# Gates in one write, a ninth offset on the other diagonal, and a router in token halves: new instruction orders in a fused vision-transformer kernel

## What is computed

```python
t = unfold3x3(x)                         # [16, 3136, 64*9]
h1 = relu(t @ W1 + b1); s = sigmoid(h1 @ W2 + b2)
h = (t * s) @ W3 + b3                    # tokenizer
h = concat([cls_tok, h])                 # 3137 tokens
u = rmsnorm(layernorm(h)); q, k, v = u @ w_qkv; q, k = elu(q) + 1, elu(k) + 1
a = layernorm(h) + (q @ sum(k v^T)) / (q @ sum(k)) @ w_out + b_out   # 8 heads of 8
h = h + a + rmsnorm(a, w_norm2)
y = layernorm(h)
top2 = top_k(softmax(relu(y @ rw1 + rb1) @ rw2 + rb2), 2); g = softmax(top2)
h = h + sum over 2 of 6 experts: g_e * (relu(relu(y @ e1) @ e2) @ e3 + b)
```

## Time and profile before

| | us |
|---|---|
| median of 3 runs (2600.67 to 2604.88) | 2604.82 |
| the profiled execution, its own time | 2603.84 |
| its span, first to last instruction | 2602.1 |
| mean granted TensorE clock (1.00 is full speed) | 0.906 |

### The profile page before, as it was taken

The page is one execution under the profiler, slowest core; times in us unless marked ns, Lnnn a source line. Parts: engine busy times, 40 slices in busy tenths (PEclk is TensorE's granted clock), DMA queues, the critical chain, the costliest instruction groups (busy, mean ns, idle before and its releaser), DMA issues. The chain is left out here.

```text
span 2602.1 us, 36855 instructions
## 1 busy us (share of the span) xinstructions
PE 2135.0 (82%) x12353; PEld 921.4 (35%) x12353; DVE 1350.6 (52%) x3631; ACT 1103.6 (42%) x2213; POOL 511.4 (20%) x346
## 2 busy tenths in 40 slices
PE   7888878888878888888888888888888888876665
PEld 2333433333333333333334333333333333333322
DVE  4454646454545555564646464646464645544442
ACT  3443434444444444343534444444444444433233
POOL 1112212121221212122212121212121212121110
PEclk9998989899999989899989998999899999977777
DMA  2112222313131312222222222232313131211122
GB/s 106 61 61 63 63 71 53 84 46 91 46 91 46 88 49 80 57 69 68 69 68 67 71 66 71 57 81 56 81 46 91 46 91 46 51 43 43 44 48 58
DMA packets 41339, 168.30 MB, mean 65 GB/s; under 512 B 6048, under 2 KB 19264, under 8 KB 33984
## 3 DMA queue, kind: packets, MB, share of 16 engines
q1 hardware_dynamic: 41152, 165.95, 23.6%
HBM read 151.87 MB, written 14.05 MB: 64 GB/s over the span
## 5 line engine op out<-in xcount | busy, mean ns | idle before, releaser
L1243 DVE TENSOR_TENSOR gh<-f,gate_sp 128x448 f32<-128x448 f32 (+1 forms) x342 | 199.8, 612 | 436.5 <-issue 360.9
L682 ACT ACTIVATE th<-ps,b_half 128x448 f32<-128x448 f32 x504 | 294.8, 630 | 171.8 <-PE ps L354 106.4
L810 ACT ACTIVATE f<-ps,packed 128x448 f32<-128x448 f32 (+1 forms) x342 | 201.1, 630 | 371.9 <-DVE gh L1243 371.2
L920 DVE SCALAR_TENSOR_TENSOR gated<-th,x_tile 128x448 f32<-128x448 f32 x504 | 301.0, 617 | 16.3 <-PE ps L370 7.9
L388 PE MATMUL ps<-packed,rx_c 112*128 112x112 f32 (+1 forms) x225 | 56.7, 407 | 303.7 <-DVE rx_c L930 303.7
L856 POOL TENSOR_TENSOR rstd_u<-var_u,exponent 112x8 f32<-112x8 f32 (+1 forms) x57 | 92.3, 1619 | 1003.2 <-DVE var_u L946 1003.2
L326 PE MATMUL ps<-x_tile,packed 128*64 128x448 f32 x896 | 256.5, 693 | 2.0 <-DMA x_tile<-x_rows 2.0
L354 PE MATMUL ps<-h,packed 64*128 64x448 f32 x896 | 229.1, 588 | 9.8 <-ACT h L674 6.9
L370 PE MATMUL ps<-gated,w_half 128*64 128x448 f32 x896 | 203.7, 557 | 34.0 <-DVE gated L920 34.0
L856 POOL TENSOR_TENSOR rms_b<-ms_b,exponent 112x8 f32<-112x8 f32 (+1 forms) x57 | 107.3, 1882 | 591.2 <-DVE ms_b L1102 591.2
L610 PE MATMUL ps<-gh,packed 128*64 128x448 f32 (+1 forms) x684 | 216.7, 731 | 5.3 <-DVE gh L1243 5.3
(11 more groups left out here) (140 smaller groups left out, 3344.1 us busy)
## 6 DMA issues: line engine op xcount, KB each, us to landing
gate_sp<-gates_d SPq DMA_DIRECT2D x112, 672.0 KB, 7.0
x_tile<-x_rows SPq DMA_DIRECT2D x56, 696.0 KB, 5.2
x_tile<-x_rows SPq DMA_DIRECT2D x56, 580.0 KB, 3.8
out<-out_t SPq DMA_DIRECT2D x56, 224.0 KB, 8.1
gates_d<-gates_c SPq DMA_DIRECT2D x224, 5.2 KB
packed<-pack SPq DMA_DIRECT2D x1, 690.0 KB, 9.8
packed<-pack SPq DMA_DIRECT2D x1, 448.0 KB, 6.5
packed<-pack SPq DMA_DIRECT2D x1, 430.0 KB, 3.6
```

The lines of the kernel that those rows point to most:

```text
L682: act.activation(th[(u + s) % 4][:, :], bank(S0 + u % 2), ACT.Tanh, bias=b2_half[:, m:m + 1], scale=0.5).then_inc(th_set, 1)
L810: act.activation(f2[j % 4][:, 0:n], bank(S0 + j % 2, n), ACT.Relu, bias=cst("eb2")[:, j:j + 1]).then_inc(f2_set, 1)
L920: dve.scalar_tensor_tensor(as_rows(gated[u % 4][:, :]), as_rows(th[(u + s) % 4][:, :]), 1.0, x_view(s, u), ALU.add, ALU.mult).then_inc(gat ...
L1243: dve.tensor_tensor(gh[j % 4][:, 0:n], f2[j % 4][:, 0:n], gate_sp[:, j, 0:n], ALU.mult).then_inc(gh_set, 1)
```

## The change

- `save_gates` is one DMA. The experts are sorted for it in the weights (`rw2`, `eb3`, `order` swap neighbours for image 1), `spread_gates` reads every second row, and `gate_hidden` picks its row accordingly.
- SyncE's order is write, output store, broadcast, x load. It was store, x load, write, broadcast.
- The ninth offset of w1, w2 and w3 takes the other diagonal of the array, for which its pixels are on the other image's partitions. center_a, q_prod, out_proj and center_b become two quadrant products each on the first diagonal.
- The router's product is made in two halves of the tokens (224 each) on four strips of 32 columns, `rh` is 128 x 224, and the logits are four products of 64 rows into two banks, M0 and D1 (banks D0 and D1 change places so that these two are neighbours). The router's bias is added on VectorE, into SBUF, which makes 21 gate operations.
- The banks' waits follow: `kv_prod` and `attention` wait for that addition in the place of `att_set` for D1, `logits` waits for `att_set`.
- The orders of all engines are new. In the diff their old lines are left out; of ScalarE's order the first part is shown.

```diff
-                for img in range(2):
-                    for low in range(2):
-                        top = (low + img) % 2
-                        sp.dma_start(gates_d[f % 2][top * E + img:top * E + E:2, 0:nt * tw],
-                                     gates_c[img * E + low:img * E + E:2, 0:nt * tw]).then_inc(gate_saved, 16)
+                sp.dma_start(gates_d[f % 2][:, 0:nt * tw], gates_c[:, 0:nt * tw]).then_inc(gate_saved, 16)
...
-                    rows = gates_d[f % 2][top * E:top * E + E, 0:n]
+                    rows = gates_d[f % 2][top:2 * E:2, 0:n]
...
+                if 1 <= step - 10 <= CLS_T: save_gates(step - 10)
+                if 1 <= step - 12 <= CLS_T: store_out(step - 12)
+                if 1 <= step - 10 <= CLS_T: spread_gates(step - 10)
+                if 3 <= step + 2 <= BLOCKS: load_x(step + 2)
...
-                        pe.matmul(as_rows(bank(L0, p0=64 * img, p1=64 * img + 64)), cst("w1", 4 * C)[half(img)],
-                                  x_view(s, UNITS - 1)[half(img)], start=False, stop=True).then_inc(w1_done, 1)
+                        pe.matmul(as_rows(bank(L0, p0=64 * img, p1=64 * img + 64)), cst("w1", 4 * C)[half(1 - img)],
+                                  x_view(s, UNITS - 1)[half(1 - img)], start=False, stop=True).then_inc(w1_done, 1)
...
-                pe.matmul(bank(L1, nt * tw), cst("center"), h_of(r, 0)[:, 0:nt * tw], start=True,
-                          stop=True).then_inc(ctr_done, 1)
+                for img in range(2):
+                    pe.matmul(ps[half(img), L1, 0:nt * tw], cst("center")[half(img)], h_of(r, 0)[half(img), 0:nt * tw],
+                              start=True, stop=True).then_inc(ctr_done, 1)
...
+                w = min(n, N // 2)
+                for part in range((nt + 1) // 2):
+                    for img in range(2):
+                        p0 = 2 * RH * part + RH * img
+                        mm = pe.matmul(ps[p0:p0 + RH, M0, 0:w], cst("rw1")[half(img)],
+                                       y[f % 2][half(img), part * w:(part + 1) * w], start=True, stop=True)
+                        if part == (nt + 1) // 2 - 1:
+                            mm.then_inc(router_done, 1)
...
+                if f + 1 <= BLOCKS:
+                    pe.wait_ge(att_set, 2 * (f + 1))
+                    pe.wait_ge(clsatt_set, (f + 1 - 1) // CHUNKS + 1)
+                elif 1 <= f - 1:
+                    pe.wait_ge(gate_step, GATE_STEPS * (f - 1 - 1) + 1)
+                for k in sorted(range(nt), key=lambda k: k % 2):
+                    mm = pe.matmul(ps[0:tw, LOGIT[k // 2], 2 * E * (k % 2):2 * E * (k % 2 + 1)],
+                                   rh[half(k // 2), k % 2 * tw:(k % 2 + 1) * tw], cst("rw2")[half(k // 2)],
+                                   start=True, stop=True)
+                    if k >= nt - 2:
+                        mm.then_inc(logit_done, 1)
...
@@ the order of TensorE @@
             for step in STEPS:
+                if 1 <= step - 9 <= CLS_T: out_proj(step - 9)
+                if 0 <= step - 2 <= BLOCKS: q_prod(step - 2); kv_prod(step - 2)
+                if 1 <= step - 1 <= BLOCKS: w2(step - 1, 3); w3(step - 1, 1); w3(step - 1, 2); w2(step - 1, 4)
+                if 1 <= step - 1 <= BLOCKS: w3(step - 1, 3)
+                if 1 <= step - 9 <= CLS_T: mean_sq_b(step - 9)
+                if 0 <= step - 2 <= BLOCKS: spread_hn(step - 2)
+                if 1 <= step - 10 <= CLS_T: gates_channels(step - 10)
+                if 1 <= step - 1 <= BLOCKS: w3(step - 1, 4)
+                if 0 <= step - 2 <= BLOCKS: kv_outer(step - 2)
                 if 1 <= step - 11 <= CLS_T: out_tokens(step - 11)
+                if 1 <= step - 10 <= CLS_T: expert_h1(step - 10, 0)
+                if 1 <= step - 8 <= BLOCKS: attention(step - 8)
                 if 1 <= step - 9 <= CLS_T: spread_b(step - 9)
+                if 1 <= step - 10 <= CLS_T: expert_h1(step - 10, 1); expert_h2(step - 10, 0)
                 if 1 <= step - 9 <= CLS_T: center_b(step - 9)
+                if 1 <= step - 10 <= CLS_T: expert_h1(step - 10, 2); expert_h2(step - 10, 1)
                 if 1 <= step - 9 <= CLS_T: var_mean_b(step - 9)
+                if 1 <= step <= BLOCKS: w1(step, 0); w1(step, 1); w1(step, 2); w1(step, 3)
                 if 0 <= step - 1 <= BLOCKS: center_a(step - 1)
+                if 1 <= step <= BLOCKS: w1(step, 4)
+                if 1 <= step - 10 <= CLS_T: expert_h2(step - 10, 2); expert_bias(step - 10)
                 if 1 <= step - 9 <= CLS_T: spread_c(step - 9)
+                if 0 <= step - 1 <= BLOCKS: var_mean_a(step - 1)
                 if 1 <= step - 10 <= CLS_T: expert_out(step - 10, 0)
+                if 1 <= step <= BLOCKS: w2(step, 0)
+                if 1 <= step - 10 <= CLS_T: expert_out(step - 10, 1); expert_out(step - 10, 2)
+                if 1 <= step <= BLOCKS: w2(step, 1)
                 if 1 <= step - 9 <= CLS_T: router(step - 9)
+                if 0 <= step - 1 <= BLOCKS: spread_u(step - 1)
                 if 1 <= step - 8 <= BLOCKS: att_channels(step - 8)
                 if 1 <= step - 9 <= CLS_T: logits(step - 9)
+                if 1 <= step <= BLOCKS: w3(step, 0); w2(step, 2)
...
@@ the order of ScalarE @@
             for step in STEPS:
                 if 1 <= step - 10 <= CLS_T: relu1(step - 10, 4); relu1(step - 10, 5); relu2(step - 10, 2)
+                if 1 <= step - 10 <= CLS_T: relu2(step - 10, 3)
+                if 0 <= step - 1 <= BLOCKS: center_a(step - 1); square_a(step - 1)
+                if 1 <= step - 10 <= CLS_T: relu2(step - 10, 4)
+                if 1 <= step <= BLOCKS: hidden(step)
                 if 1 <= step - 10 <= CLS_T: relu2(step - 10, 5)
+                if 1 <= step <= BLOCKS: gate_tanh(step, 0); gate_tanh(step, 1); gate_tanh(step, 2)
                 if 1 <= step - 9 <= CLS_T: router_relu(step - 9)
+                if 1 <= step <= BLOCKS: gate_tanh(step, 3)
                 if 1 <= step - 8 <= BLOCKS: att_copy(step - 8)
+                if 1 <= step <= BLOCKS: gate_tanh(step, 4); gate_tanh(step, 5)
+                if 0 <= step - 1 <= BLOCKS: exp_q(step - 1)
+                if 1 <= step - 9 <= CLS_T: gate_exp(step - 9)
...
+                if 1 <= step - 19 <= CLS_T: rstd_b_(step - 19)
+                if 0 <= step - 11 <= BLOCKS: rstd_u_(step - 11); rstd_h_(step - 11)
+                if 1 <= step - 18 <= CLS_T: sum_b_(step - 18); rms_b_(step - 18); block_out(step - 18)
...
+                    halves = (nt + 1) // 2
+                    dve.wait_ge(logit_done, 2 * (f - 1) + min(nt, 2))
+                    dve.tensor_tensor(logit.rearrange("p (b c) -> p b c", b=halves),
+                                      ps[0:tw, LOGIT[0]:LOGIT[halves - 1] + 1, 0:w // halves],
+                                      cst("rb2")[0:tw, 0:w].rearrange("p (b c) -> p b c", b=halves),
+                                      ALU.add).then_inc(gate_step, 1)
+                    so_far(1)
...
@@ the order of VectorE @@
             for step in STEPS:
+                if 0 <= step - 2 <= BLOCKS: sum_kv(step - 2)
+                if 1 <= step - 9 <= CLS_T: spread_b(step - 9); rms_normed(step - 9)
+                if 1 <= step - 8 <= BLOCKS: denominators(step - 8, 0); denominators(step - 8, 1); inverses(step - 8)
+                if 1 <= step - 8 <= BLOCKS: cls_attended(step - 8)
+                if 1 <= step - 9 <= CLS_T: variance_b(step - 9)
+                if 1 <= step - 8 <= BLOCKS: attended(step - 8, 0); attended(step - 8, 1)
                 if 1 <= step - 9 <= CLS_T: spread_c(step - 9)
+                if 1 <= step - 10 <= CLS_T: gate_hidden(step - 10, 0); gate_hidden(step - 10, 1)
                 if 1 <= step - 10 <= CLS_T: gate_hidden(step - 10, 2); gate_hidden(step - 10, 3)
+                if 0 <= step - 1 <= BLOCKS: deviations_a(step - 1)
+                if 1 <= step - 10 <= CLS_T: gate_hidden(step - 10, 4); gate_hidden(step - 10, 5)
+                if 0 <= step - 1 <= BLOCKS: scales_a(step - 1)
                 if 1 <= step - 9 <= CLS_T: normed_b(step - 9)
+                if 1 <= step <= BLOCKS: gate_pixels(step, 0)
+                if 1 <= step - 10 <= CLS_T: result(step - 10)
+                if 0 <= step - 1 <= BLOCKS: spread_u(step - 1)
+                if 1 <= step <= BLOCKS: gate_pixels(step, 1); gate_pixels(step, 2)
                 if 0 <= step - 1 <= BLOCKS: normed_u(step - 1)
                 if 1 <= step - 9 <= CLS_T: gates_part(step - 9, 0)
                 if 0 <= step - 1 <= BLOCKS: spread_hn(step - 1)
                 if 1 <= step - 9 <= CLS_T: gates_part(step - 9, 1)
+                if 1 <= step <= BLOCKS: gate_pixels(step, 3)
+                if 1 <= step - 9 <= CLS_T: gates_part(step - 9, 2)
+                if 1 <= step <= BLOCKS: gate_pixels(step, 4)
+                if 1 <= step - 9 <= CLS_T: gates_part(step - 9, 3)
+                if 1 <= step <= BLOCKS: gate_pixels(step, 5)
+                if 1 <= step - 9 <= CLS_T: gates_part(step - 9, 4)
```

(11 more changed lines are left out.)

## The result

The changed kernel takes 2064.99 us (median of 4 runs, 2057.39 to 2068.59) where the kernel before took 2602.74 beside it: ratio 0.7931, 95% interval 0.7906 to 0.7956. The profiled execution took 2064.24 us, its span is 2062.5.

A forecast was written before the change was run, and what follows sets the result against it. The bound was taken as the chain gate copy, four writes, broadcast, gating 0, spread copy, transpose. From 2603.84 us, 354 for full steps and 38 for the tail were taken: 2212, on the median 2213; range 2107 (a little less) to 2375.

The forecast's parts named there:

- The gap: TensorE's 5.42 us wait before transposing the second layer norm's spread reciprocal goes, and the full step's clock becomes 1.00.
- TensorE's own work: Floor of a full step from TensorE's work alone: 32.9 us, or 34.2 if quadrants don't overlap.
- the new step is 15.8 + 19.4 + 1.1 = 36.3 us: Full step: first half led by TensorE 15.8, second led by VectorE 19.4, unplaced waits 1.1; 44.0 before.
- short waits for copies and sums: First half of the step: TensorE waits 0.4 for spread_b's copy, 0.6 for center_b's sum, 0.3 for relu1; 1.3 us.
- a sign of being wrong that the prediction names: In the full step, the reduction sums_a waiting behind a gating would show the forecast wrong; no size given.
- short waits that I can't place: Full step: today's waits of 0.70 and 0.40 us before two tokenizer products, added again as 1.1 us.
- VectorE as the leader: VectorE leads the step's second half: 18.2 us from sums_a to normed_hn's end, 19.4 to the next expert_h1(0).
- The gates' margin: Gates land 11.7 us after the first expert product, TensorE's expert_out(0) wants them at about 15; margin 3 us, nothing priced.
- gates late: Rival: gates land at 17.5 us, expert_out(0) waits 3 us, clock falls; 40.5 us a step, 2406 in all; chance 0.18.
- the 2.1 us of issue: Dropping three of four gate writes saves 2.1 us of issue; nothing taken from it in full steps, bounds 0 and 2.1.
- The tail: Steps behind the full ones, 33.56 us each, lose 3.8 net; some 10 steps, 38 us less (bounds 25 and 50).
- TensorE leads throughout: Rival: in full steps a good order fills the forecast's waits; 34.0 us a step, 2107 us in all; chance 0.10.

The follow-up runs named there:

- old_w1_ahead: Kernel before, with VectorE's spread copy moved ahead of the gating of experts 0 and 1, and TensorE's w1(0) to w1(3) ahead of spread_c: 2350.61 us.
- xb_extra_dve: x_behind_broadcast with three more copies on VectorE in the second half of the step, which nobody reads: 2064.08 us, ratio 0.7933.
- x_behind_broadcast: Changed kernel with each block's x load issued one step later, behind the gates' broadcast instead of ahead of the gate write: 2039.56 us, ratio 0.7830.

## Why the prediction was wrong

**The gap: right.** The transpose has no wait, clock 1.00, and old_w1_ahead shows the cause by doing the two moves alone. It is also most of what was forecast: 5.3 us a step of the forecast's 7.7.

**TensorE's own work: right, and it was the answer.** 32.9 forecast, 33.22 measured. The pair center_a and w1(4) takes 0.80 us, so its four quadrant products pass in about the time of one; undoing it costs 0.68 of work, forecast 0.89. Undoing router and logits costs 0.75, forecast 0.45 + 0.3. The Trainium skill, TensorEngine Tiling (Array Packing), Gotcha 1: PSUM Pressure, by which the halves in one bank would take turns, is contradicted by these runs too: center_a's halves lie on different rows and share bank L1.

**The sum of waits: this failed.** The step that failed is "the new step is 15.8 + 19.4 + 1.1 = 36.3 us", 3.4 us of idleness over the work, where 0.53 was there. From expert_h1(0) (1244.41) to sums_a (1259.40) it is 14.99, not 15.8: of the 1.3 us of short waits for copies and sums some 0.1 is seen, since TensorE has other work queued before it comes to them. The reduction sums_a itself starts 0.96 us behind its transposes (1258.44) and not 0.68, because the gating runs until 1259.48; that is a sign of being wrong that the prediction names. From sums_a to the end of normed_hn (1276.93) it is 17.53, not 18.2; from there to the next step 1.39 and not 1.2; and the 1.1 us of "short waits that I can't place" did not come. Together 0.81 + 0.67 - 0.19 + 1.1 = 2.4 us, from 36.3 to the 33.9 of this one step; the mean step is 33.75.

**VectorE as the leader: wrong.** A term was mis-sized. Two small operations, gs_dif and g_w, took long where they stood, beside a power and a sum on POOL; moved, they are short. Before, in the order of time:

```profile
1202.67 1.95 POOL L856 TENSOR_TENSOR rms_b<-ms_b,exponent 112x8 f32<-112x8 f32 x1 [9.04 <-DVE ms_b L1102]
1203.04 1.09 DVE L1211 SCALAR_TENSOR_TENSOR gs_dif<-g_exp,gs_inv 112x8 f32<-112x8 f32 x1
1204.59 1.20 POOL L878 TENSOR_TENSOR sum_b<-ring,h 128x448 f32<-128x448 f32 x1
1205.24 0.61 DVE L1216 TENSOR_TENSOR g_w<-g_e,packed 112x48 f32<-112x48 f32 x1
```

The same two over the run (ns least, median, longest), before and after:

```profile
L1211 DVE SCALAR_TENSOR_TENSOR gs_dif<-g_exp,gs_inv x57: 150/1091/1096, 228.4 to 2587.0; 112x8 f32<-112x8 f32 x56, 8x2 f32<-8x2 f32 x1
L1216 DVE TENSOR_TENSOR g_w<-g_e,packed x57: 159/610/1100, 230.6 to 2587.3; 112x48 f32<-112x48 f32 x56, 8x12 f32<-8x12 f32 x1
```

```profile
L1238 DVE SCALAR_TENSOR_TENSOR gs_dif<-g_exp,gs_inv x57: 150/256/853, 223.9 to 2050.6; 112x8 f32<-112x8 f32 x56, 8x2 f32<-8x2 f32 x1
L1243 DVE TENSOR_TENSOR g_w<-g_e,packed x57: 157/201/210, 225.7 to 2050.8; 112x48 f32<-112x48 f32 x56, 8x12 f32<-8x12 f32 x1
```

By the medians this is 1.24 us a step less; VectorE's total falls by 1.06 (23.74 to 22.68), the new bias add being in it. xb_extra_dve bears on the rest: with 1.3 us more a step still grows by 0.48 only.

**The gates' margin: mechanism right, who wants them first wrong.** I wrote that "TensorE wants it for expert_out(0) at about 15. So a margin of 3 us for TensorE, and nothing is priced". They came at 12.84, not 11.7, and expert_out(0) at 14.6 had no wait. But relu2(4) wants a buffer that gating frees, and relu2(5), which w2(0) waits for, stands behind it in ScalarE's queue. The margin was measured at one consumer only. The missing price was small: x_behind_broadcast shows it as 0.46 us a step. The rival "gates late" named the right limit with a price (4.2 us a step) nine times too high. The "nothing" taken of the 2.1 us of issue (bounds 0 and 2.1) holds better: four writes cost 0.37 a step.

**The tail: 62 and not 38.** Of 6.23 us a step (33.56 to 27.33) 0.7 lie between copy and gating, where 1.3 was forecast, for there part b's copy took over. The other 5.5 lie behind the gating (20.13 to 14.59), where 2.5 was forecast: 2.1 up to the last expert_out, 0.9 in router and logits, 1.85 in VectorE's gate operations (g_w took 1.10 beside POOL's power and g_d 1.02 beside its sum, where now gs_dif alone takes 0.85, beside the sum) and 0.7 from the last gate operation to the copy. Of these the third and the fourth were in no term of mine.

**The cases.** "TensorE leads throughout" (34.0 a step, 2107) is nearest to what happened, with 33.75 and a better tail and start, though the gates' loop still held 0.46 of the step; I gave it 0.10. Against it I set "18 of these lie in one half", a walk's sum, where "VectorE's total is 23.62 us a step" was a row and spoke for it.

## What to carry to other kernels

Copies and reductions that TensorE needs do not belong in an in-order queue behind work that waits for a trip through DRAM; two such moves were worth 253 us here. A small write whose landing somebody waits for is issued ahead of a bulk load, and the load behind the read (1.5 us instead of 5.0). When waits found by a walk are added to an engine's work, compare with the busiest engine's own work: here every other engine had a third of its time free and other work was queued in between, and the step (33.75) came out near that work (33.22) and not near the sum (36.3). A margin has to be checked on every queue that the late result passes, not only on the last one.

## What was not expected of the hardware

- The small write behind the x load of 1276 KB let its reader go 5.0 us after its issue, without the load 1.54. The Trainium skill, DMA: Bandwidth & Descriptors, Queues, rings and completion order, says that a semaphore increment lands only after every earlier write from that SDMA engine; the two times agree with it. Whether only the write's report is late, or its packets wait behind the load's as well, no run here tells.
- A VectorE operation of 112 x 8 elements (gs_dif) took 1.09 us where it fell into a POOL power, and 0.26 after the move; that power took 1.95 and 1.65. The Trainium skill, GPSIMD Engine Reference, Specifications, says that POOL shares its SBUF interfaces with VectorE and contends with instructions that have two SBUF inputs; gs_dif, g_w and g_d have two. The Trainium skill gives no size there. In the traces it is no fixed factor but the rest of POOL's operation: beside a POOL sum the stretched operation ends 0.01 to 0.07 us behind the sum's end (g_w 47 and g_d 7 times before, gs_dif 55 times after), and beside the power rms_b 0.38 to 0.50 us ahead of the power's end (gs_dif 47 times, g_w 7). Gs_dif is short now, and it starts 0.23 us before a sum ends (1271.57 and 1271.80 in the step above). That contention is the cause fits these ends, but no run changes it alone.
- Two products of two quadrants each, on opposite diagonals, pass in 0.80 us, hardly more than the 0.76 between neighbours of one shape; each pair's halves share a bank.
